# The second cross attention: transfers in order of need, V of the second batch made beside the first heads, shift rows loaded, shift constant as bias

## The reference

```
scores = einsum('bhqd,bhkd->bhqk', qh, kh) / sqrt(32)
causal = arange(1024)[None, :] <= arange(512)[:, None] + 512
attn   = softmax(where(causal, scores, -10000.0))
x      = layernorm(x + einsum('bhqk,bhkd->bhqd', attn, vh))
```

## Time and profile before

| what | value |
|---|---|
| time, median of 3 runs | 2242.52 us (2238.49 to 2245.76) |
| the profiled execution's own time | 2239.3 us |
| its span | 2237.5 us |
| TensorE busy | 1955.8 us (87%) |
| VectorE busy | 1435.1 us (64%) |
| ScalarE busy | 1058.4 us (47%) |
| GpSimd busy | 596.9 us (27%) |
| the phase `phase_cross1` in the trace | from 1562.6 us to about 1860 us |

### The profile page before, as it was taken

How to read it: one execution, slowest core, us unless ns; L and a number is a source line. 1 busy time by engine, 2 the same in 40 slices (tenths; PEclk the granted TensorE clock), 3 DMA queues, 4 the chain that set the end, 5 groups by cost and what they waited for, 6 DMA issues and landing times. The chain is left out here.

```text
span 2237.5 us, 36241 instructions
## 1 busy us (share of the span) xinstructions
PE 1955.8 (87%) x12872; PEld 1195.2 (53%) x12872; DVE 1435.1 (64%) x2728; ACT 1058.4 (47%) x2118; POOL 596.9 (27%) x510
## 2 busy tenths in 40 slices
PE   7888878978999799986999999997688886899998
PEld 4555544446777477773544545454255562355553
DVE  4666665366775667766856658487699966545334
ACT  3666634232333323331645537274599892344332
POOL 3555500022332323310100101011555550132320
PEclk8999988988999899998999999999599967999999
DMA  4000003021110211104002010000910003476533
GB/s 138 25 25 1 1 1 132 24 64 33 47 47 0 73 34 40 44 0 138 20 20 57 20 38 19 0 1 7 220 23 2 2 2 132 146 193 175 137 71 90
DMA packets 96111, 125.46 MB, mean 56 GB/s; under 512 B 9296, under 2 KB 52560, under 8 KB 95968
## 3 DMA queue, kind: packets, MB, share of 16 engines
q1 hardware_dynamic: 89248, 107.79, 16.0%
q0 software_dynamic: 6720, 15.73, 3.8%
HBM read 101.67 MB, written 18.61 MB: 54 GB/s over the span
## 5 line engine op out<-in xcount | busy, mean ns | idle before, releaser
L1170 POOL TENSOR_TENSOR wl<-stage,wh 128x512 fp32r<-128x512 f32 x80 | 117.3, 1497 | 395.8 <-DVE wh L1161 395.8
L1429 POOL TENSOR_TENSOR Zl<-z,Zh 128x512 f16<-128x512 f32 x32 | 51.1, 1597 | 494.1 <-ACT Zh L1590 494.1
L77 PE MATMUL PS<-XTh,wh 128*128 128x512 f16 x416 | 159.4, 383 | 19.8 <-ACT t L2013 19.0
L1270 ACT ACTIVATE h<-PS,bup 128x512 f32<-128x512 f32 x64 | 44.2, 690 | 278.4 <-PE PS L79 278.4
L78 PE MATMUL PS<-XTl,wh 128*128 128x512 f16 x416 | 159.3, 383 | 0.0
L79 PE MATMUL PS<-XTh,wl 128*128 128x512 f16 x416 | 159.2, 383 | 0.0
L2636 ACT ACTIVATE P<-PS 128x512 f32<-128x512 f32 (+3 forms) x256 | 144.1, 563 | 18.5 <-PE PS L2573 15.4
L2637 ACT ACTIVATE PTh<-PS 128x512 f16<-128x512 f32 (+3 forms) x256 | 145.7, 569 | 0.0
L2482 POOL TENSOR_TENSOR PTl<-P,PTh 128x512 f16<-128x512 f32 (+2 forms) x128 | 112.3, 888 | 105.4 <-ACT PTh L2637 105.3
L2651 DVE TENSOR_REDUCE M<-PS 128x1 f32<-128x640 f32 (+3 forms) x128 | 126.9, 1011 | 4.2 <-PE PS L2555 4.2
L2573 PE MATMUL PS<-QS,KS 98*128 98x512 f16 (+3 forms) x256 | 99.0, 387 | 27.7 <-ACT PTh L2637 16.1
(11 more groups left out here) (377 smaller groups left out, 6022.8 us busy)
## 6 DMA issues: line engine op xcount, KB each, us to landing
stage<-in_ffn_W SPq DMA_DIRECT2D x18, 1024.0 KB, 5.3
stage<-in_ffn_Wg SPq DMA_DIRECT2D x9, 1024.0 KB, 5.4
stage<-in_ffn_Wup SPq DMA_DIRECT2D x16, 512.0 KB, 3.9
stage<-in_ffn_Wdn SPq DMA_DIRECT2D x16, 512.0 KB, 3.7
wq<-in_attn_wq SPq DMA_DIRECT2D x4, 1024.0 KB, 6.7
C<-in_ctx SPq DMA_DIRECT2D x8, 512.0 KB, 9.2
stage<-in_ffn_Wsw SPq DMA_DIRECT2D x16, 256.0 KB, 3.5
stage<-in_attn_WV SPq DMA_DIRECT2D x16, 256.0 KB, 4.0
```

Of the source, the lines that this page charges most:

```text
L77: pe.matmul(out, a[0], b[0], start=start, stop=False, skip_group_check=True)
L1170: nc.gpsimd.tensor_tensor(piece(wl[q], ch), piece(st, ch), plain(piece(wh[q], ch)), ALU.subtract).then_inc(w_lo, 1)
```

## The change

Context tiles are loaded raw into KS[1], read there as 16 tiles of float32 (`stage`), in order of need: stacks of the first group, the two constants, the eight context tiles of batch 0, the second group, the shift column of batch 0, the eight context tiles of batch 1, the last two groups. V of batch 0 is made before the loop, V of batch 1 inside it, one tile after each of the first eight heads. The scaling step moves from ScalarE to GpSimd. Since KS[1] is the stage, the stacks of batch 1 are issued only after the last tile of V. The two memsets of KS become transfers of a constant into two partitions. The three-step shift parts become two, the constant log(1024) is added as a bias of the exponential, and the waits of TensorE on `m_shift` become waits on `m_lo`.

```diff
         @block.sync
+            def context(b):
+                for t in range(b * CT, (b + 1) * CT):
+                    sp.dma_start(stage[:, t * D:(t + 1) * D],
+                                 c.inp["ctx"][b, (t % CT) * P:(t % CT + 1) * P, :]).then_inc(ctx_in[t], 16)
+            def shift_column(b):
+                sp.dma_start(KS[b][R:R + 2].rearrange("p h s -> p (h s)").bitcast(F32), c.inp["c_shift"]).then_inc(shift_in[b], 16)
...
+            stacks(0, (0,))
             for to, name in ((tri32, "c_tri"), (triT32, "c_triT")):
                 sp.dma_start(to[:], c.inp[name]).then_inc(const_in, 16)
-            stacks(0)
-            for t in range(B * CT):
-                need(sp, v_lo, t - SLOTS + 1)
-                sp.dma_start(P32[:, t % SLOTS, :], c.inp["ctx"][t // CT, (t % CT) * P:(t % CT + 1) * P, :]).then_inc(ctx_in[t % SLOTS], 16)
+            context(0)
+            stacks(0, (1,))
+            shift_column(0)
+            context(1)
+            stacks(0, (2, 3))
             shift_rows(0)
-            stacks(1)
-            for g in range(1, N // GS):
+            shift_rows(1)
+            shift_rows(2)
+            sp.wait_ge(v_lo, B * CT)
+            shift_column(1)
+            stacks(1, range(4))
+            for g in range(3, N // GS):
                 shift_rows(g)
...
         @block.gpsimd
+            nc.gpsimd.memset(grow[:], float(np.log(PS_))).then_inc(grow_done, 1)
             nc.gpsimd.memset(V[:, :, :, 2 * DV:VW], XS).then_inc(ones_done, 1)
             pool.wait_ge(ones_done, 1)
-            nc.gpsimd.memset(KS[0][R:P].bitcast(F32), two_shifts).then_inc(ones_done, 1)
-            for t in range(B * CT):
-                pool.wait_ge(v_hi, 2 * t + 2)
-                nc.gpsimd.tensor_tensor(V[:, t, :, 0:DV], P32[:, t % SLOTS, :].rearrange("p (h e) -> p h e", h=H),
-                                        V[:, t, :, DV:2 * DV], ALU.subtract).then_inc(v_lo, 1)
-            pool.wait_ge(v_lo, B * CT)
-            nc.gpsimd.memset(KS[1][R:P].bitcast(F32), two_shifts).then_inc(ones_done, 1)
+            def v_low(t):
+                pool.wait_ge(v_hi, t + 1)
+                nc.gpsimd.tensor_scalar(raw(t), raw(t), XS, None, ALU.mult).then_inc(v_scaled, 1)
+                pool.wait_ge(v_scaled, t + 1)
+                nc.gpsimd.tensor_tensor(V[:, t, :, 0:DV], raw(t), V[:, t, :, DV:2 * DV], ALU.subtract).then_inc(v_lo, 1)
+            for t in range(CT):
+                v_low(t)
...
                     for kt in ON_POOL:
                         low_part(pool, nc.gpsimd, n, kt, lo_pool)
+                if n < CT:
+                    v_low(CT + n)
                 if n >= 2:
                     add(n - 2)
...
         @block.tensor
-                if n == H and kt == 0:
-                    pe.wait_ge(ones_done, 3)
+                if n % H == 0 and kt == 0:
+                    pe.wait_ge(shift_in[b], 16)
...
-                    pe.wait_ge(m_shift, 1 + sum(turn_group(i) is not None for i in range(n + 1)))
+                    pe.wait_ge(m_lo, 1 + sum(turn_group(i) is not None for i in range(n + 1)))
+                if kt == 0 and n % H == 0:
+                    pe.wait_ge(v_lo, CT * (b + 1))
...
-            pe.wait_ge(ones_done, 2)
-            pe.wait_ge(v_lo, B * CT)
...
         @block.scalar
-            for t in range(B * CT):
-                act.wait_ge(ctx_in[t % SLOTS], 16 * (t // SLOTS + 1))
-                nc.scalar.activation(V[:, t, :, DV:2 * DV], P32[:, t % SLOTS, :].rearrange("p (h e) -> p h e", h=H),
-                                     ACT.Copy, scale=XS).then_inc(v_hi, 1)
-                nc.scalar.activation(P32[:, t % SLOTS, :], P32[:, t % SLOTS, :], ACT.Copy, scale=XS).then_inc(v_hi, 1)
-            act.wait_ge(v_lo, B * CT)
+            def v_high(t):
+                act.wait_ge(ctx_in[t], 16)
+                nc.scalar.activation(V[:, t, :, DV:2 * DV], raw(t), ACT.Copy, scale=XS).then_inc(v_hi, 1)
+            act.wait_ge(ones_done, 1)
+            for t in range(CT):
+                v_high(t)
+            act.wait_ge(grow_done, 1)
...
+                    nc.scalar.activation(P32[:, i % SLOTS, cols], c.PS[:, 4 + i % 2, cols], ACT.Exp, bias=grow[:],
+                                         scale=SC)
...
+                if n < CT:
+                    v_high(CT + n)
...
         @block.vector
-                nc.vector.tensor_scalar(mt[:], turned_bank(n), 1.0 / MS, -float(np.log(PS_)) / SC / MS,
-                                        ALU.mult, ALU.add).then_inc(m_shift, 1)
-                dve.wait_ge(m_shift, g + 1)
                 need(dve, m_in, 32 * g)
-                nc.vector.tensor_copy(mh[:], mt[:]).then_inc(m_hi, 1)
+                nc.vector.tensor_scalar(mh[:], turned_bank(n), 1.0 / MS, None, ALU.mult).then_inc(m_hi, 1)
                 dve.wait_ge(m_hi, g + 1)
-                nc.vector.tensor_tensor(ml[:], mt[:], mh[:], ALU.subtract).then_inc(m_lo, 1)
+                nc.vector.scalar_tensor_tensor(out=ml[:], in0=turned_bank(n), scalar=1.0 / MS, in1=mh[:], op0=ALU.mult,
+                                               op1=ALU.subtract).then_inc(m_lo, 1)
```

More of the change, by code:

```diff
@@ L2430, in phase_cross1 @@
         M = sb("M", [P, N // GS, GS, QT], F32)
-        mt = sb("mt", [GS * QT, P], F32)
+        grow = sb("grow", [P, 1], F32)
         mh, ml = sb("mh", [GS * QT, P], F16), sb("ml", [GS * QT, P], F16)
@@ L2437, in phase_cross1 @@
         const_in, const_done = sem("const_in"), sem("const_done")
-        ctx_in = [sem(f"ctx{i}_in") for i in range(SLOTS)]
+        ctx_in = [sem(f"ctx{t}_in") for t in range(B * CT)]
+        shift_in = [sem(f"shift{b}_in") for b in range(B)]
         v_hi, v_lo = sem("v_hi"), sem("v_lo")
-        ones_done = sem("ones_done")
+        ones_done, grow_done, v_scaled = sem("ones_done"), sem("grow_done"), sem("v_scaled")
         s_done, max_done = sem("s_done"), sem("max_done")
-        m_turned, m_shift, m_hi, m_lo, m_in = sem("m_turned"), sem("m_shift"), sem("m_hi"), sem("m_lo"), sem("m_in")
+        m_turned, m_hi, m_lo, m_in = sem("m_turned"), sem("m_hi"), sem("m_lo"), sem("m_in")
         e_done, exp_done = sem("e_done"), sem("exp_done")
@@ L2448, in phase_cross1, with raw @@
         block = ctx.enter_context(nc.Block())
-        two_shifts = float(np.full(2, -MS, np.float16).view(np.float32)[0])
+        stage = KS[1][:].rearrange("p h s -> p (h s)").bitcast(F32)
+        def raw(t):
+            return stage[:, t * D:(t + 1) * D].rearrange("p (h e) -> p h e", h=H)
         def head(n):
@@ L2486, in _, with stacks @@
         def _(sp):
-            def stacks(b):
-                for h4 in range(4):
+            def context(b):
[4 more added lines that the diff above has]
+                sp.dma_start(KS[b][R:R + 2].rearrange("p h s -> p (h s)").bitcast(F32), c.inp["c_shift"]).then_inc(shift_in[b], 16)
+            def stacks(b, groups):
+                for h4 in groups:
                     rows = slice(h4 * DV, (h4 + 1) * DV)
@@ L2515, in _ @@
         def _(pool):
+            nc.gpsimd.memset(grow[:], float(np.log(PS_))).then_inc(grow_done, 1)
             nc.gpsimd.memset(V[:, :, :, 2 * DV:VW], XS).then_inc(ones_done, 1)
             pool.wait_ge(ones_done, 1)
-            nc.gpsimd.memset(KS[0][R:P].bitcast(F32), two_shifts).then_inc(ones_done, 1)
-            pool.wait_ge(ones_done, 2)
-            for t in range(B * CT):
-                pool.wait_ge(v_hi, 2 * t + 2)
-                nc.gpsimd.tensor_tensor(V[:, t, :, 0:DV], P32[:, t % SLOTS, :].rearrange("p (h e) -> p h e", h=H),
-                                        V[:, t, :, DV:2 * DV], ALU.subtract).then_inc(v_lo, 1)
-            pool.wait_ge(v_lo, B * CT)
-            nc.gpsimd.memset(KS[1][R:P].bitcast(F32), two_shifts).then_inc(ones_done, 1)
-            pool.wait_ge(ones_done, 3)
+            def v_low(t):
[5 more added lines that the diff above has]
+                v_low(t)
             def add(n):
@@ L2635, in _ @@
                     need(act, z_done, i + 1 - RING)
-                    nc.scalar.activation(P32[:, i % SLOTS, cols], c.PS[:, 4 + i % 2, cols], ACT.Exp, scale=SC)
+                    nc.scalar.activation(P32[:, i % SLOTS, cols], c.PS[:, 4 + i % 2, cols], ACT.Exp, bias=grow[:],
+                                         scale=SC)
                     nc.scalar.activation(PTh[:, i % RING, cols], c.PS[:, 4 + i % 2, cols], ACT.Exp,
-                                         scale=SC).then_inc(exp_done, 1)
+                                         bias=grow[:], scale=SC).then_inc(exp_done, 1)
+                if n < CT:
+                    v_high(CT + n)
             for t in range(NT):
@@ L2755, in constants @@
         "c_tri": causal,
+        "c_shift": np.full((2, H * S2), -32.0, np.float16).view(np.float32),
         "c_triT": causal.T,
```

## The result

The changed kernel takes 2270.17 us (median of 4, 2265.41 to 2273.33), the one before 2244.14 in the same comparison: a ratio of 1.0121, interval 1.0096 to 1.0145. It is slower by 26 us by the medians and 27 by the ratio, far outside the range of 2235.5 to 2249.0. The profiled execution took 2265.41 us, 26.1 more than before's.

A forecast was written before the change was run, and what follows sets the result against it. It took VectorE and ScalarE together to bound the loop, with only the gap ahead idle. Terms -6.3 + 3.3 + 1.5 + 0.5 = -1.0 us gave 2241.5 us, range 2235.5 to 2249.0.

The forecast's parts named there:

- The bias costs nothing: In the loop's exponentials: the added bias operand costs 0, as the instruction is there anyway.
- No rival: Rivals: sharing costs little, 0.22; queue doesn't clear, 0.20; sharing compounds, 0.08; moved loop start doesn't show, 0.04.
- The gap: Idle time ahead of the loop: V made in the lead starts the loop earlier, gain 6.3 us, bounds 4.5 and 8.9.
- my slow bound: Shift column's transfer ahead of the loop: 2.6 us if one engine carries each row; the gain would be 5.0.
- V in the loop: First eight heads: GpSimd's added steps make VectorE stand, cost 3.3 us, bounds 1.6 and 8.8.
- Shift parts: Loop's turned maxima: TensorE waits for ml, 0.3 us later in five heads, cost 1.5 us.
- the upper bound: Shift parts: TensorE's longer standstills may lower the clock; if in all five heads, 3.5 us more.
- VectorE's saved 0.25 us: Shift parts' lower bound: if VectorE is the bound there, two steps save 5 x 0.25, so -1.3 us.
- Stacks of batch 1: Later issue in the loop: stacks just in time for head 16, group 3's shift rows near head 12; 0.5 us, at most 3.
- the four terms: The gap -6.3, V in the loop +3.3, shift parts +1.5, stacks of batch 1 +0.5: sum -1.0 us.

The follow-up runs named there:

- e2: The kernel before with only the bias operand added to the exponentials and the constant taken out of mt; 2271.25 us, ratio 1.0131.
- e1: The changed kernel without its bias, the constant back in three-step shift parts; 2242.5 us, ratio 0.9996 to the kernel before.
- e8b: e1 without GpSimd's scaling step, so the output is not the reference's; 2235.82 us, ratio 0.9978 to the kernel before.
- e7b: The kernel before with the bias operand on one of each tile's two exponentials only; 2250.75 us, ratio 1.0053.
- e4: e3 with the first shift rows issued ahead of the stacks of groups 2 and 3; 2238.63 us, ratio 0.9980 to the kernel before.
- e3: e1 with all 16 tiles of V made ahead of the loop, scaling on ScalarE; 2238.33 us, ratio 0.9986 to the kernel before.
- e6b: e5b with two-step shift parts, the wait for ml and the constant in a third loaded row; 2232.73 us, ratio 0.9959 to the kernel before.
- e5b: e4 with group 1's shift rows issued between two halves of batch 1's stacks; 2226.99 us, ratio 0.9943 to the kernel before.

## Why the prediction was wrong

**The failed step** is the last sentence of the part on the stacks: "The bias costs nothing: it's an operand of an instruction that is there anyway." It measured 29.5 us in e2, alone, and 28 us between the changed kernel and e1, with the two-step parts and 1.3 us of the table load in it. Each of the 512 exponentials makes the next one start 0.09 us later, 1.4 us a head, of which 1.1 reach the head's time (8.04 against 6.93), as ScalarE had only 0.28 us to spare. No rival had it, and the range had no bound for it, though the trace of before had the row. There, in the second layer's self-attention, ScalarE's timeline has two activations of the same size with a bias operand (bq) back to back:

```profile
1338.03 0.69 ACT L1576 ACTIVATE q<-PS,bq 128x512 f32<-128x512 f32 x1
1338.60 0.70 ACT L1578 ACTIVATE Qh<-PS,bq 128x512 f16<-128x512 f32 x1
```

They start 0.57 us apart. They aren't exponentials, so the row alone was a hint and not a proof. In the phase itself, without the operand, it's 0.47:

```profile
1626.28 0.60 ACT L2636 ACTIVATE P<-PS 128x512 f32<-128x512 f32 x1
1626.75 0.62 ACT L2637 ACTIVATE PTh<-PS 128x512 f16<-128x512 f32 x1
```

The Trainium skill (ScalarE: Activation LUTs, What ACT_TABLE_LOAD costs) states it outright: each pointer operand of one value per partition adds about 93 ns. The runs agree: 0.57 - 0.48 = 0.09. From the rows alone the term would have been 16 x 0.09 - 0.28 = 1.2 us a head, 37 us for 32 heads and 2279 in all. That is above what was measured, as plain heads grew by 1.1 and a head with turned maxima by less (8.45 against 7.72 in e2).

**ScalarE as the bound** then undid other terms. With 8.04 us a head VectorE had over a microsecond of idle time (17.13 busy of 20), so in the changed kernel V cost only ScalarE's own part: heads 4, 5, 6 and 8 take 8.35 to 8.48 us, 0.3 to 0.45 more, for which the high half of V on a ScalarE that is never idle accounts. So this kernel says nothing on the wait of VectorE that I forecast; e1 does.

**The gap**: predicted 6.3 us of gain, measured 4.8 from the first transfer (45.8 to 41.0), in e1 4.2. Mechanism and place were right: the shift rows landed last, at 1602.05 where I had 1602.2. But the phase had begun 1.6 us earlier in that execution, so the way there took 41.0 us, and my sum had 39.6 (1602.2 less 1562.6). The missing 1.4 us are the queue's end, which isn't as I put it. Most large transfers were through by some 1598, and then, where I had 1.3 us for the shift column and 1.7 for the rows, 4 us passed with the DMA engines hardly used:

```profile
1596.00:1598.00 2.00, 0.14 (x2) 0.00 (x0) 1.43 (x2) 0.00 (x0) 0.00 (x0) 0.50 0.95 193
1598.00:1600.00 2.00, 0.00 (x0) 0.00 (x0) 0.00 (x0) 0.00 (x0) 0.00 (x0) 0.50 0.24 65
1600.00:1602.00 2.00, 0.00 (x0) 0.00 (x0) 0.00 (x0) 0.00 (x0) 0.00 (x0) 0.50 0.04 14
```

The packets in the changed kernel's trace show what holds that tail. Each shift row goes as 16 packets of 256 B. Thirty of the 32 packets of the two rows had started by 1599.81, but the last two started at 1601.13 and 1601.15, right behind packets of 1 and 2 KB that had run one after another, with hardly anything else moving, until 1601.12. So neither the rows nor the column were being moved in that time: the last stacks were, on a DMA engine that was late with its share, and the rows' last packets stood behind them. Where such lateness can come from shows in the same trace. The shift column went as two packets of 32 KB side by side, of 2.94 and 3.13 us (from 1579.16 and 1579.45), so two engines each had some 3 us more to do than the others. That is near my slow bound of 2.6 us, by which the gain would have been 5.0, and not the 1.3 that I took. The Trainium skill's rule that I cited there (two engines for this transfer) is borne out. From at least 14 engines busy with packets of 1 KB and more to none it took 3.7 us here and 4.3 in e1 and e8b, but 1.9, 1.3 and 1.5 behind batch 1's stacks in before, e2 and e7b, which have no column. That the late engine is one of the column's two is not shown, and batch 1's column (2.2 to 2.4 us) was followed by only 1.9 us in the changed kernel, so part of the tail stays open. That the rows wait behind the stacks is also shown by e4, where the wait is gone when they are issued first.

**V in the loop**: predicted 3.3 us, 5 heads of 7.7. Without the bias e1 shows heads of 7.3 to 7.8 and 3.7 us over the first ten marks, against before as against e3. The size is near, but partly by luck: the scaling was mis-sized, 1.49 us for my 0.7 and beyond the bound, and it doesn't hold VectorE up itself, it only delays the subtraction that does. VectorE's standing until a GpSimd subtraction is over is shown in e1 and e8b.

**Shift parts**: predicted +1.5 us, bounds -1.3 and +5. Measured in e6b against e5b: 0.31 us more for each wait, as forecast, and 3.6 us in all by the ratio, part of it by the clock, as the upper bound had it. e6b also has the third row, which no run takes apart from the shift parts, but heads without turned maxima take 6.93 us in it. That VectorE's saved 0.25 us would rule is refuted.

**Stacks of batch 1**: no wait of TensorE for KS near head 10 in the changed kernel, as predicted; but its heads are longer, so this doesn't test the margin. e1 has heads of 6.93 us there, and its timeline of TensorE shows the term that I had put at 0.5, the rows of group 3 late behind batch 1's stacks: at the start of head 12 it waited for them.

```profile
1694.51 0.39 PE L2594 MATMUL PS<-QS,KS 98*128 98x512 f16 x1 [1.25 <-DMA QS<-ml]
```

That head took 8.82 us by ScalarE's marks (1692.74 to 1701.56), before 6.92: it is the one after the head with turned maxima. So the whole wait came on top, and with what followed it cost 1.9 us, where I had 0.5 and at most 3.

Without the bias the four terms were worth -1.0 us by my sum, and -2.5 without the shift parts, which e1 lacks too. e1 measured +0.7 by the medians and -0.9 by the ratio. That this is so near is luck in part. In e1's profiled execution the gap gained 2.1 us less than forecast (4.2 for 6.3), V cost 0.4 more and the late rows 1.4 more; against these stand the 1.35 us of the table load, which my sum didn't have.

## What to carry to other kernels

An edit that adds only an operand can still have a price: look for a row with that operand and one without, and compare the distance of starts, not the durations, which overlap. Multiply it by the count on the engine with the least idle time before calling it free. When transfers are reordered, list what each later waiter needs and when, for the whole time that the queue stays full: e4 won 6.7 us at the loop's start and lost 7.6 four heads later through the same queue.

## What the runs showed of the hardware

- With a bias operand the next activation starts 0.57 us after one of 512 columns instead of 0.48 (e7b). At 128 columns it is 0.25 (1754.57 to 1754.82, changed kernel) instead of 0.17 (1754.55 to 1754.72, kernel before), so the price is nearly the same for a quarter of the columns.
- GpSimd's scaling in place of 128x512 float32 by a constant took 1.49 us (changed kernel). Its subtraction of two such tiles took 1.13 at its shortest in the kernel before, and 1.20 to 1.27 at the median in the loops of the changed kernel and e1, beside VectorE's low parts.
- A VectorE low part (two inputs) that began during a GpSimd subtraction ended 0.54 to 0.55 us after it, in 16 of 16 cases (e1, changed kernel). One that began in the last 0.1 to 0.4 us of GpSimd's scaling took 0.67 to 0.69 us, in 14 of 14, as beside an idle GpSimd (0.68 in e8b).
- Loading ScalarE's table for the exponentials took 1.28 us in each of these kernels.
- A row of 4 KB that lands in 1.7 us in an empty queue took 8 us in the changed kernel, in which 0.94 MB were moved (8.06 us at 117 GB/s), and 13 us in e4, in which 2.06 MB were moved (12.95 at 159). The end of that was slow: 65 and 14 GB/s in the last two stretches of 2 us in the changed kernel, 68 in the last 4.5 us in e4.
- A row of 4 KB was moved in 16 packets of 256 B, and TensorE was released 0.9 us after the last of them (1601.16 to 1602.05). A transfer of 64 KB in two partitions was moved in two packets that ran side by side for 2.94 and 3.13 us.
